# Moving the attention value product's copies and low parts ahead of other work in a fused attention and quantised feed-forward kernel

## What is computed

```python
q = (x @ Wq).reshape(B, S, HEADS, DIM_HEAD)...     # x is layernorm(x) here
k = (context @ Wk)...;  v = (context @ Wv)...
attn = softmax(einsum('bhsd,bhld->bhsl', q, k) * scale)
x = x + einsum('bhsl,bhld->bhsd', attn, v)... @ Wo + bo
# feed-forward, on layernorm(x):
xq = act_fake_quant(x, clip_x)                     # one scale for the whole tensor
gate = xq @ weight_fake_quant(w_gate).T            # one scale for each weight row
up   = xq @ weight_fake_quant(w_up).T
h = act_fake_quant(silu(gate) * up, clip_down)     # again one scale for the whole tensor
x = x + h @ weight_fake_quant(w_down).T
```

## Time and profile before

| | us |
|---|---|
| median of 3 runs | 534.18 (533.76 to 534.37) |
| the profiled execution | 534.28 |
| its span on the core | 532.49 |
| granted clock of TensorE over the span | 1.00 of full |

### The profile page before, as it was taken

One profiled execution on the slowest core, in us unless ns is written; L12 is line 12 of the kernel. 1 busy time (PEld: TensorE's weight loads), 2 busy tenths in 40 slices (PEclk: granted clock), 3 DMA queues, 4 the chain that ended last, 5 costly groups with the idle time before them and its releaser, 6 DMA issues.

```text
span 532.5 us, 7840 instructions
## 1 busy us (share of the span) xinstructions
PE 523.9 (98%) x2659; PEld 352.8 (66%) x2666; DVE 448.7 (84%) x808; ACT 288.9 (54%) x416; POOL 229.4 (43%) x347
## 2 busy tenths in 40 slices
PE   8999999999999999999999999999999999999997
PEld 8888788787888888888777644444444445444444
DVE  4968798989989899898899689998999988776663
ACT  4844645565465654554435745545554543999300
POOL 4397679688596886866454000000000000055332
PEclk9999999999999999999999999999999999999999
DMA  8946365846667566435959984842243021499997
GB/s 307 315 180 183 112 180 187 285 155 211 221 196 245 182 224 190 153 111 169 224 84 353 247 207 180 319 120 44 77 118 94 26 41 30 163 334 209 135 111 127
DMA packets 82941, 93.81 MB, mean 176 GB/s; under 512 B 47085, under 2 KB 50157, under 8 KB 82645
## 3 DMA queue, kind: packets, MB, share of 16 engines
q1 hardware_dynamic: 77877, 84.13, 51.5%
q0 software_dynamic: 4320, 7.87, 9.9%
q10 hardware_dynamic: 704, 1.31, 0.8%
HBM read 47.51 MB, written 37.78 MB: 160 GB/s over the span
## 4 chain that ended last, share of the span: by engine, by line
PE 91%; DVE 4%; DMA 2%; issue 1%; SPq 1%; ACT 1%; POOL 0%; DVEq 0%
PE SP L653 14%; PE QO L648 14%; PE SP L450 6%; PE QO L415 4%; PE QO L414 4%; PE QO L413 4%; PE SP L693 4%; PE PTP L693 4%; PE QO L693 4%; PE PTP L483 3%; PE WOP L523 2%; PE WOP L525 2%; PE WOP L524 2%; PE MI L525 2%; PE MI L523 2%; PE MI L524 2%
## 5 line engine op out<-in xcount | busy, mean ns | idle before, releaser
L1599 POOL DMA_DIRECT2D out<-n2b x30 | 28.0, 974 | 204.6 <-DVE n2b L1410 204.5
L936 ACT ACTIVATE sil<-QO,fsc 128x512 f32<-128x512 f32 x87 | 59.8, 687 | 72.2 <-PE QO L648 71.3
L648 PE MATMUL QO<-nT,wgu 128*128 128x512 bf16 x340 | 87.2, 379 | 0.0
L653 PE MATMUL SP<-nT,wgu 128*128 128x512 bf16 x340 | 87.2, 379 | 0.0
L1357 DVE SCALAR_TENSOR_TENSOR h<-SP,fsc,sil 128x512 f32<-128x512 f32 x87 | 65.3, 750 | 16.1 <-PE SP L653 14.1
L1492 POOL TENSOR_TENSOR PN<-P,rs 128x512 f32<-128x512 f32 x64 | 44.6, 719 | 41.6 <-DVE rs L1019 41.6
L1363 DVE TENSOR_REDUCE hmx<-h 128x1 f32<-128x512 f32 x88 | 59.9, 685 | 2.9
L653 PEld LDWEIGHTS SP<-nT,wgu 128*128 128x128 bf16 x340 | 33.3, 98 | 40.1
L648 PEld LDWEIGHTS QO<-nT,wgu 128*128 128x128 bf16 x340 | 33.3, 98 | 40.1
L758 ACT ACTIVATE P<-P,r 128x616 f32<-128x616 f32 x32 | 25.9, 811 | 52.6 <-DVE P L1010 52.6
L965 ACT ACTIVATE h<-h,g 128x1536 int8<-128x1536 f32 (+2 forms) x38 | 44.3, 1262 | 0.0
(11 more groups left out here) (256 smaller groups left out, 1199.7 us busy)
## 6 DMA issues: line engine op xcount, KB each, us to landing
xTr<-in_xT SPq DMA_DIRECT2D x8, 1024.0 KB, 7.2
xn<-in_x SPq DMA_DIRECT2D x32, 256.0 KB, 4.0
out<-x SPq DMA_DIRECT2D x32, 256.0 KB, 3.1
n_rows<-n SPq DMA_DIRECT2D x32, 256.0 KB, 2.9
n2b<-n_rows SPq DMA_DIRECT2D x32, 256.0 KB, 3.6
out<-n2b POOLq DMA_DIRECT2D x30, 256.0 KB, 5.6
h_spill<-h SPq DMA_DIRECT2D x2, 2816.0 KB, 8.6
h<-h_spill SPq DMA_DIRECT2D x6, 768.0 KB, 8.0
```

The costliest lines, as they stand in the source:

```text
L648: mm = e.matmul(QO[:, at:at + 512], wgu_v[:, k, cols(ic)], nT[:, b % 2, :, k, :], start=(k == 0), stop=(k == 3))
L653: mm = e.matmul(SP[:, at:at + 512], wgu_v[:, k, cols(NI + ic)], nT[:, b % 2, :, k, :], start=(k == 0), stop=(k == 3))
L936: e.activation(sil[:, n % SR, :], QO[:, (n % 2) * 512:(n % 2) * 512 + 512], ACT.Silu, scale=fsc[:, ic:ic + 1]).then_inc(silu, 1)
```

## The change

Five movements, no instruction added or removed.

- ACT: in stages 2 to 6 `PV_high(b - 1)` runs ahead of `normed(s - 6)`; in stage 1 `w_round(2)`, which had its place ahead of the loop, runs behind `PV_high(0)`. Behind the loop, `normed(22)` moves from ahead of `PV_high(6)` to behind `PT_high(28)`.
- DVE: ahead of the loop, the statistics of input tiles 5 and 6 move up in front of `PT_low(3)` and of `w_top(2)`; `v_low(4)` moves from ahead of `w_top(2)` to behind `PV_low(0)` in stage 1.
- POOL: `w_integer(2)` moves behind the scales and biases of tiles 5 and 6.
- SP: `load_n2(0)` moves from behind `store_x1(28)` to behind `store_n2(25)`.

```diff
@@ ACT @@
             v_high(4)
-            w_round(2)
             for b in range(1, 7):
                 s = 4 * b
+                PV_high(b - 1)
                 if b > 1:
                     normed(s - 6)
-                PV_high(b - 1)
+                else:
+                    w_round(2)
                 PT_high(s)
...
-            normed(22)
             PV_high(6)
             PT_high(28)
+            normed(22)
             soft_exp(29)
@@ DVE @@
             soft_sub(4)
+            first_stats(5)
+            first_aggr(5)
             PT_low(3)
             soft_sum(4)
             soft_rec(4)
-            v_low(4)
+            first_stats(6)
+            first_aggr(6)
             w_top(2)
             w_scale(2)
             w_inverse(2)
-            first_stats(5)
-            first_aggr(5)
-            first_stats(6)
-            first_aggr(6)
...
                 PV_low(b - 1)
                 if b > 1:
                     largest(s - 7)
+                else:
+                    v_low(4)
@@ POOL @@
             soft_norm(4)
-            w_integer(2)
             for n in (5, 6):
                 first_scale(n)
             for n in (5, 6):
                 first_bias(n)
+            w_integer(2)
@@ SP @@
             store_n2(25)
+            load_n2(0)
             store_n2(26)
             for n in range(28, NT):
                 store_n2(n - 1)
                 store_x1(n)
-                if n == 28:
-                    load_n2(0)
```

## The result

The changed kernel took 537.49 us, median of four executions (536.85 to 538.22), against 534.17 (533.76 to 534.37, four executions) for the kernel before: a ratio of 1.0066, 95% interval 1.0053 to 1.0078. It is slower by 3.3 us; 536.3 was predicted, with 533.0 to 539.0 as the range. The profiled execution is the one of 538.22 us, its span 536.4 against 532.5, so its rows have to account for 3.9 us. Two of the four executions had the full clock over the whole span and took 536.85 and 536.86; the two others, the profiled one among them, had 0.996 and 0.997 and took 538.11 and 538.22.

The account below looks back on a forecast made before the run. PE, busy 98% of the span, was taken as the bound. Costs of 3.3 us less gains of 1.2 took the profiled 534.28 to 536.4, or 536.3 for the median; range 533.0 to 539.0.

Parts of the forecast that it names:

- S(5), gain 0.89: Scores S(5) in stage 1: with ACT copying ahead of w_round(2), PE's wait for the low parts goes, 0.89 us.
- S(29) and the reload: End of first half: moving normed(22) saves S(29)'s wait, 0.85 us; earlier load_n2(0) saves the tile reload's wait, 0.33.
- Stage 1, PT(7) +1.1: Late store_w(2) holds SP's queue, load_w(5) leaves 3.0 us late, PT(7) comes 1.1 us later, S(5)'s gain included.
- the chain from there: From w_top through w_round, split_hi, PT_high and PT_low to PE's next PT: at least 6.1 us.
- S(9), +0.6: PE at S(9) waits another 0.6 us for DVE, left late by stage 1; bounds 0.2 and 0.8.
- Stages 2 to 6: Late store_n2 delays SP's weight loads: PE loses 0.2 us in stage 2, 0.9 in 4, 0.5 in 5, otherwise nothing.
- The 3.0 us of SP's delay: Stages 2 to 6: last copy, normed and three issues put load_vb and everything behind it 3.0 us later.
- With PE ahead by some gain, SP's waits are ahead by the same: Stages 2 to 6: PE's earlier gains move SP's waits equally, so the predicted delays there stay unchanged.
- Only the gains: Rival: the loads have more room than read and PE never meets their delay; 532.1 us, chance 15%.
- It compounds: Rival: stages 1, 2, 4 and 5 pay upper bounds, DVE's lateness passes on; 538 to 539.3 us, chance 15%.
- The queue: SP issues in order with nothing overtaking, so a late store holds the loads behind it for its full wait.

Follow-up runs that it names:

- Experiment 3: Against the kernel before: w_round(2) behind PV_high(0) alone, 535.46 us; with earlier statistics and both edits between the halves, 533.35; those two edits alone, 532.64.
- the tail alone: The kernel before with only normed(22) moved behind PT_high(28) and load_n2(0) issued earlier: 532.64 us, ratio 0.9977.
- experiment 4: The changed kernel with ten unread products on PE in the gap ahead of PT(7): 537.00 us, ratio 1.0060.
- experiment 1: The changed kernel in stages 2 to 6, with normed(s - 6) back ahead of the copies, 534.89 us; or with only store_n2(s - 6) behind load_vb(b), 534.83.
- v_low back: The changed kernel with v_low(4) put back ahead of w_top(2) on DVE: 536.53 us, ratio 1.0055.
- rounding only: The kernel before with only w_round(2) moved behind PV_high(0) on ACT: 535.46 us, ratio 1.0027.

## Why the prediction was right, point by point

The forecast was +2.1 us against a measured +3.3, inside its range and on its side. Part of that is luck: S(9) cost nothing, stages 2 to 6 paid at other places than said, and a wait that was missed in stage 1 and half a cause at S(5) happened to cost the sum nothing. Its steps:

- **S(5), gain 0.89: right in size (-1.01), half of the cause.** The step puts the wait down to ACT, which "ran w_round(2) until 65.51 while pairs 2 and 3 stood finished", and names DVE's statistics only as work that moves along. Experiment 3 shows that the statistics held the low parts as long, and that freeing ACT alone gains nothing. The change did both, so the number came out.
- **S(29) and the reload, gains 0.85 and 0.33: right.** Without the change's other parts the tail alone made the feed-forward half start 1.7 us sooner, 0.5 more than the sum of the two. Most of that lies in how the waits were read. The idle time in the brackets counts from the end that the profile gives to the product before, and less than the whole delay shows in it: from the first product of WOP to the first of MI, in the reload, PE took 293.05 - 291.85 = 1.20 us before and 296.74 - 296.31 = 0.43 in the changed kernel, so this wait was worth 0.77 us and not 0.33.
- **Stage 1, PT(7) +1.1: right in mechanism, too small.** It measured +1.82. load_w(5) left at 82.01 (81.5 said) and w_top(5) began at 85.04 (84.4 said); the chain from there took 6.17 us (6.1 said). The step named two reasons for the late store_w(2), v_low(4) and the bias pair ahead of w_integer(2), and missed a third, w_round(2) behind the copies. In the changed kernel the bias pair is the last of the three (69.3) and the missed one the first (68.2), so the sum did not suffer; the expectations of the single-step runs, which put the named two back, did (533.3 expected, 535.48 measured).
- **S(9), +0.6: wrong.** PE waited for nothing there. DVE was late by less than PE, which had lost 3.4 us by then.
- **The clock, not in the sum: +1.6 at its place, +1.3 in half of the executions.** This is a missing term, worth 0.6 of the median; without it the measured time is +2.7 against the +2.1 forecast. An idle time of 2.6 us ahead of PT(7) follows from the step's own reasoning: PE, 1.0 ahead by the gain at S(5), would reach PT(7) early and wait for all of it. The prediction gave the lateness of PT(7) and not the length of the gap, and so had no place where to ask what the clock would do.
- **Stages 2 to 6, +0.2, 0, +0.9, +0.5: 1.6 in sum against 2.35 measured, but at other places.** From S(9) to S(25) the shift grew by 0.63, 0.61, 0.34 and 0.77. The 3.0 us of SP's delay was too much: in stage 4 of the changed kernel load_vb(4) was 2.3 us late from PT(16) on, load_w(17) 1.7, and against PE behind its own new wait 1.0. DVE's wait of 2 to 3 us came in stages 5 and 6 and not in stage 4. PE met the delay not at PT(19) and PT(23), but at the next stage's head, mostly through the load of an input tile. The prediction followed load_w(s + 1) to the first who wanted it and not to what stands behind the weight's store in SP's own queue.
- **"With PE ahead by some gain, SP's waits are ahead by the same": right for what waits on PE alone.** The loads that were late did not all move with PE. Products in the gap (experiment 4) saved 1.6 us at S(9) and had kept 0.8 at the feed-forward half, in the profiled executions.
- **The rivals.** "Only the gains" was to give 532.1. The gains without the two moves on DVE and POOL that the prediction charged gave 533.35, and the reason is the rounding: DVE waited 1.64 us for load_w(5) in that run too, so the loads do not have the room of this rival. "It compounds" (538 and more) is nearest to the executions with the lower clock, by another mechanism than the one it told.
- **The queue.** The prediction leaned on SP's rows, which show nothing overtaking. The two runs of experiment 1 bear it out: the same order on ACT costs 2.7 us with the store ahead of load_vb and nothing behind it. The Trainium skill, "DMA: Bandwidth & Descriptors", section "Anatomy of one DMA — SWDGE (gpsimd) path", says that the issuing sequencer does the waiting; these runs agree with that.

## What to carry to other kernels

Where a step is moved behind other work, follow all that hangs on it to every queue in which something waits for it, and then what stands behind that wait in the same queue: here one 0.8 us step on ACT held a store, the store held twelve issues of 10 us, and these held the weight and the input tile that the critical path wanted. Ask of a gap in PE not only how late it makes the next step but how long it is. A step that is moved to free one engine pays only where that engine alone was late. Test each moved step alone: of the movements here, the two around the end of the first half carried all of the gain that lasted, as far as these runs can tell, and a kernel with these two alone (532.64 us) is faster than the kernel before and the one with all five.

## What the runs showed of the hardware

- **A gap of 2.2 to 2.6 us in PE's work can be followed by 3 to 4 us at half the clock, 1.6 us of PE's time.** Three profiled executions show it (gaps of 2.63, 2.40 and 2.22 us), one with a gap of 2.27 does not. The four kernels concerned lost clock in 2 of 4, 2 of 5, 8 of 11 and 4 of 11 executions, so the length of the gap alone doesn't decide it. With ten unread products in the gap none of five executions lost it. The fall cost 1.3, 0.0, 0.6 and 0.7 us of the whole time, by the medians of either sort.
- **What an issue holds SP for is no constant.** The same load, a weight tile of w_down of 704 KB, held it for 0.43, 0.62, 0.94 and 1.65 us in different kernels, and from store_w(2) to load_w(5) it took from 11.76 us (v_low back) to 13.5 (rounding only), with the same instructions. A delay summed from the rows of one trace carries about 1 us of uncertainty here.
